# The last block of an expert layer moved into the head of the next block, with the layernorm and the turns done tile by tile

## The reference, cut to what matters

```python
# experts (end)
out = shared + acc @ Wup.T            # shared = (x2 @ sw1.T * sqrelu(x2 @ swg.T)) @ sw2.T
x = x + out
# linear attention (start)
h = _layernorm(x)                     # (x - mean) / sqrt(var + 1e-5), per token
qkv = silu(h @ qkv_w.T)               # 32 heads of 64, q, k, v
gate = sigmoid(h @ gate_w.T)
...
```

## Time and profile before

| | |
|---|---|
| median of 3 runs | 2136.52 us (2131.28 to 2137.3) |
| the profiled execution's own time | 2135.23 us |
| its span, first to last instruction | 2133.4 us |
| PE busy | 1935.3 us (91% of the span) |
| DVE busy | 1168.6 us (55%) |
| ACT busy | 635.2 us (30%) |
| POOL busy | 219.6 us (10%) |

### The profile page before, as it was taken

One profiled execution on the slowest core, in us unless ns is written; L12 is line 12 of the kernel. 1 busy time (PEld: TensorE's weight loads), 2 busy tenths in 40 slices (PEclk: granted clock), 3 DMA queues, 4 the chain that ended last, 5 costly groups with the idle time before them and its releaser, 6 DMA issues. The chain is left out here.

```text
span 2133.4 us, 24875 instructions
## 1 busy us (share of the span) xinstructions
PE 1935.3 (91%) x9621; PEld 1409.3 (66%) x9624; DVE 1168.6 (55%) x2069; ACT 635.2 (30%) x1013; POOL 219.6 (10%) x185
## 2 busy tenths in 40 slices
PE   7899795899997599979999999999899998899996
PEld 6677783444433458847886886877758744688885
DVE  5412737555543345547674684665643378656653
ACT  3311322444444055514340331322224221222110
POOL 0000001111201100000120120210200001112221
PEclk9999896899998599999999999999999999999998
DMA  5100402222210500014221313203202100110101
GB/s 198 40 1 0 158 11 67 67 68 58 64 37 1 158 0 1 1 36 140 77 79 66 114 54 116 97 20 117 80 31 70 60 20 22 58 37 25 39 1 40
DMA packets 67125, 124.12 MB, mean 58 GB/s; under 512 B 8512, under 2 KB 26944, under 8 KB 65472
## 3 DMA queue, kind: packets, MB, share of 16 engines
q1 hardware_dynamic: 67008, 122.53, 18.1%
HBM read 88.82 MB, written 14.68 MB: 49 GB/s over the span
## 5 line engine op out<-in xcount | busy, mean ns | idle before, releaser
L941 DVE TENSOR_REDUCE b_nm<-ps 128x1 f32<-128x1024 f32 x128 | 151.5, 1220 | 118.8 <-PE ps L862 118.8
L929 ACT ACTIVATE b_pr<-ps 128x512 f32<-128x512 f32 x256 | 132.3, 605 | 159.5 <-PE ps L880 159.5
L229 PE MATMUL ps<-d_x_high,d_w_high 128*128 128x512 f32 x384 | 154.8, 403 | 4.4 <-DVE d_w_low L1767 4.4
L230 PE MATMUL ps<-d_x_low,d_w_high 128*128 128x512 f32 x384 | 150.4, 392 | 0.0
L231 PE MATMUL ps<-d_x_high,d_w_low 128*128 128x512 f32 x384 | 150.3, 392 | 0.0
L892 PE MATMUL ps<-b_pr,b_VS 128*64 128x512 f32 x512 | 130.6, 634 | 0.0
L1544 PE MATMUL ps<-d_wo,d_ga 128*128 128x512 f32 x256 | 110.6, 593 | 1.5 <-DVE d_ga L1745 1.5
L880 PE MATMUL ps<-b_qS,b_kS 98*128 98x512 f32 x256 | 92.3, 442 | 20.1 <-DMA b_qS<-b_nm_parts 17.7
L862 PE MATMUL ps<-b_kS,b_qS 96*128 96x512 f32 x256 | 95.0, 461 | 15.6 <-DMA b_qS<-b_q_parts 10.1
L880 PEld LDWEIGHTS ps<-b_qS,b_kS 98*128 98x128 f32 x256 | 44.1, 192 | 90.7 <-issue 52.1
L1659 POOL TENSOR_TENSOR d_sqsum<-d_sqsum,d_sq 128x512 f32<-128x512 f32 x32 | 42.4, 1325 | 487.4 <-ACT d_sq L1604 487.2
(11 more groups left out here) (372 smaller groups left out, 4592.5 us busy)
## 6 DMA issues: line engine op xcount, KB each, us to landing
b_kS<-b_k_parts SPq DMA_DIRECT2D x96, 128.0 KB, 2.3
f_rows<-d_fw SPq DMA_DIRECT2D x24, 512.0 KB, 3.0
f_w<-f_rows SPq DMA_DIRECT2D x12, 1024.0 KB, 4.8
b_qS<-b_q_parts SPq DMA_DIRECT2D x96, 64.0 KB, 2.0
a_convT<-in_convT SPq DMA_DIRECT2D x4, 1024.0 KB, 12.8
b_ctxT<-in_ctxT SPq DMA_DIRECT2D x8, 512.0 KB, 5.1
d_w<-in_d_wq SPq DMA_DIRECT2D x16, 256.0 KB, 4.4
d_w<-in_d_wk SPq DMA_DIRECT2D x16, 256.0 KB, 4.3
```

What stands on the lines that cost most here:

```text
L229: nc.tensor.matmul(out, lhsT[0], rhs[0], start=start, stop=False)
L230: nc.tensor.matmul(out, lhsT[0], rhs[1], start=False, stop=False)
L929: nc.scalar.activation(pr[:, n % RING, :], c.ps[:, 4 + n % BANKS, :], ACT.Exp).then_inc(exp_done, 1)
L941: nc.vector.tensor_reduce(nm[:, g % 2, u:u + 1], c.ps[:, banks:banks + 2, :], AX.XY, ALU.max, negate=True).then_inc(job_read, 1)
```

## The change

Block 2 leaves `experts` and becomes the head of block 5. The blocks 3 and 4 vanish as blocks: their loads stand at the head of SP's list in block 5, and the layernorm is done by tile with `TileNorm`.

```diff
 experts():
-    a_turned, a_moved, out_done, added = (c.sem(f"c_{n}") for n in ("a_turned", "a_moved", "out_done", "added"))
-    with nc.Block() as block:
...
+    c.experts = acc, accF, sF, s2T, wupT
 linear_attention():
+    acc, accF, sF, s2T, wupT = c.experts
+    norm = TileNorm(c, "d_ln")
+    def x_bank(t):
+        return c.ps[:, 2 + t % 2, :].rearrange("p (k t) -> p k t", k=KD)
...
             sp.dma_start(nw[:], c.dram["d_nw"]).then_inc(in_c, 16)
-            pair_weights(sp, 0)
-            group_values(sp, 0)
-
-    norm_and_split(c, "d_ln", *x_parts)
-
-    with nc.Block() as block:
-        @block.sync
-        def _(sp):
             for p in range(PAIRS):
-                if p >= 1:
-                    pair_weights(sp, p)
+                pair_weights(sp, p)
...
                     if g == 0:
                         sp.dma_start(wo[:], tiled(c.dram["d_woT"])[:, 0:GP, :]).then_inc(in_o, 16)
+                        sp.wait_ge(out_done, TT)
+                        group_values(sp, 0)
...
         @block.tensor
+            def turn_x(t):
+                pe.wait_ge(norm.normed, t + 1)
+                if t >= 2:
+                    pe.wait_ge(x_low, t - 1)
+                for k in range(KD):
+                    last = nc.tensor.transpose(x_bank(t)[:, k, :], c.xn[:, t, k * P:(k + 1) * P], c.ident[:])
+                last.then_inc(x_turned, 1)
+            def experts_output(t):
...
             def project(j, i, n):
+                if j < 2:
+                    pe.wait_ge(x_low, 4 * (n + 1))
...
-            queries_keys(0, 0, 4)
+            for n in range(2):
+                for i in range(4):
+                    last = nc.tensor.transpose(c.ps[:, n, i * P:(i + 1) * P], acc[:, 4 * n + i, :], c.ident[:])
+                last.then_inc(acc_turned, 1)
+            for t in range(TT):
+                experts_output(t)
+                if t >= 2:
+                    turn_x(t - 2)
+            queries_keys(0, 0, 1)
+            turn_x(TT - 2)
+            turn_x(TT - 1)
+            queries_keys(0, 1, 4)
             gates(0)
             values(0)
         @block.scalar
+            for n in range(2):
+                act.wait_ge(acc_turned, n + 1)
+                nc.scalar.activation(accF[:, n * BANK:(n + 1) * BANK], c.ps[:, n, :], ACT.Copy).then_inc(acc_moved, 1)
             for i in range(3):
                 high_weights(0, i)
+            for t in range(TT):
+                act.wait_ge(x_turned, t + 1)
+                nc.scalar.activation(tile_of(x_parts[0], t), x_bank(t), ACT.Copy).then_inc(x_high, 1)
             high_values(0)
             pair(0)
         @block.gpsimd
+            for t in range(TT):
+                norm.root_pool(pool, t)
         @block.vector
             for i in range(3):
                 low_weights(0, i)
+            for t in range(TT):
+                dve.wait_ge(out_done, t + 1)
+                nc.vector.tensor_tensor(c.x[:, t, :], c.ps[:, 4 + t % 4, :], c.x[:, t, :], ALU.add).then_inc(added, 1)
+                dve.wait_ge(added, t + 1)
+                norm.measure_dve(dve, t)
+                if t >= 1:
+                    norm.scale_dve(dve, t - 1)
+                if t >= 3:
+                    low_x(t - 3)
+            norm.scale_dve(dve, TT - 1)
+            for t in range(TT - 3, TT):
+                low_x(t)
+            round_weights(2)
             low_values(0)
             for i in range(3):
                 low_weights(1, i)
-            round_weights(2 * UNITS_FIRST)
+            round_weights(2 * UNITS_FIRST - 2)
```

More of the change, by code:

```diff
@@ L1391, in group_values, with tile_of @@
         sp.dma_start(wv[:], tiled(c.dram["d_wvT"])[:, :, g * DM:(g + 1) * DM]).then_inc(in_v, 16)
+    acc, accF, sF, s2T, wupT = c.experts
+    acc_turned, acc_moved, out_done, added = (c.sem(f"c_{n}") for n in ("acc_turned", "acc_moved", "out_done", "added"))
+    x_turned, x_high, x_low = (c.sem(f"d_{n}") for n in ("x_turned", "x_high", "x_low"))
+    norm = TileNorm(c, "d_ln")
+    def tile_of(part, t):
+        return part[:, :, t * P:(t + 1) * P]
+    def x_bank(t):
+        return c.ps[:, 2 + t % 2, :].rearrange("p (k t) -> p k t", k=KD)
     with nc.Block() as block:
@@ L1451, in _ @@
         def _(pe):
+            def turn_x(t):
[6 more added lines that the diff above has]
+            def experts_output(t):
+                pe.wait_ge(acc_moved, 1 + t // 4)
+                if t >= 4:
+                    pe.wait_ge(added, t - 3)
+                for k in range(2):
+                    nc.tensor.matmul(c.ps[:, 4 + t % 4, :], sF[:, k, t * P:(t + 1) * P], s2T[:, k, :],
+                                     start=k == 0, stop=False)
+                nc.tensor.matmul(c.ps[:, 4 + t % 4, :], accF[:, t * P:(t + 1) * P], wupT[:], start=False,
+                                 stop=True).then_inc(out_done, 1)
             def project(j, i, n):
@@ L1772, in low_values, with low_x @@
                 nc.vector.tensor_tensor(wv_parts[1][:], wv[:], wv_parts[0][:].bitcast(F32), ALU.subtract).then_inc(wv_low, 1)
+            def low_x(t):
+                dve.wait_ge(x_high, t + 1)
+                nc.vector.tensor_tensor(tile_of(x_parts[1], t), x_bank(t), tile_of(x_parts[0], t).bitcast(F32),
+                                        ALU.subtract).then_inc(x_low, 1)
             for i in range(3):
                 low_weights(0, i)
+            for t in range(TT):
[11 more added lines that the diff above has]
+            round_weights(2)
             low_values(0)
```

## The result

| | before | after |
|---|---|---|
| median of the runs made side by side | 2133.9 us (4 runs, 2130.99 to 2137.3) | 2118.45 us (4 runs, 2117.53 to 2120.57) |
| ratio, with its 95% interval | | 0.9919 (0.9903 to 0.9936) |
| the profiled execution's own time, its span | 2135.23, 2133.4 us | 2120.57, 2118.7 us |
| PE busy | 1935.3 us | 1932.7 us |

The kernel is faster by 15.5 us between the medians; the forecast was a gain of 15.0 us, on the other median of before. The two profiled executions are 14.7 us apart in their spans.

What follows compares the result with a forecast made beforehand. PE was taken as the bound, with waits of 13.2 and 4.4 us before the projections. 14.2 us earlier at `values(0)` plus 0.8 gave 15.0 us: 2120.2 on the profiled execution, 2121.5 as median; range 2115 to 2129 us.

Steps and rivals of the forecast that it cites:

- Block end: At the merged block's start: SP and PE begin 0.9 us after DVE's last addition, costing 0.6 us.
- DVE's start: Before the first addition to x: pair 0's weights' loads and low parts delay it to 932.8 us, from near 929.
- PE's first wait: Before tile 0's turn, behind tile 2's output: PE waits 2.7 us for the scaling, in place of 13.2.
- The steady part: Interleaved outputs and turns: 3.0 us per output and turn, DVE wants 2.8, plus 0.5 us for close waits.
- The margin: Interleaved tiles: the needed scaling and low part come from DVE's round t-1, in time with 0.2 us to spare.
- The late load: Before projection 2: `d_wv` lands 6.4 us after issue, ACT's work behind it makes PE wait 1.6 us.
- The low part of `d_wv`: On DVE behind one 8.1 us unit of quantising: ends at 969.1 us, hidden with 4.9 us to spare before `values(0)`.
- Behind `values`: At DVE's first mask product: two quantising units remain instead of three, so PE's 0.8 us loss vanishes.
- given back later: Rival after `values(0)`: loads or quantising that don't move along lose 1 to 4 us of the gain; chance 0.05.
- low clock in a rival: Rival: PE's clock falls in the interleaved part; partly, 2 to 8 us, chance 0.08; for all of it, 2142.8 us, 0.05.
- the prediction's own sign: Wrong if the interleaved stretch's clock is below 1, outputs stand 4 us apart, or `values(0)` waits for `d_wv`'s low part.
- The account: Stretch up to `values(0)`: 25.0 us removed (waits, 1.7 low clock), 11.0 paid (barrier, late start, turns, waits, ACT).

Runs made afterwards that it cites:

- x_wv_late: The changed kernel with the value weights' load issued behind pair 1's five loads instead of ahead of them; 2125.78 us, ratio 0.9955 to the kernel before.
- x_low_late: The changed kernel with pair 0's weights' low parts moved from ahead of DVE's first addition to behind later tiles; run twice, 2112.04 and 2113.5 us.
- x_order: x_low_late with queries and keys of the first half projected before the second half, ACT and DVE work reordered to match; 2113.17 us, ratio 0.9900.
- x_merge: The changed kernel with blocks merged, but layernorm done for all eight tiles at once and turns behind all outputs; 2123.92 us, ratio 0.9952.
- x_turns_one: The changed kernel with turns one tile behind the outputs in place of two; 2151.15 us, ratio 1.0085 to the kernel before.

## Why the prediction was right, point by point

- **The gain.** 15.0 us forecast, 15.5 measured between medians. 2118.45 lies 3.1 us below the forecast, and 2.6 of that are the median of before, which came out at 2133.9 beside it in place of 2136.5. That it is so close is in part luck: the sum left out 1.7 us of low clock and put 1.3 too much on the late load, and the one pair of profiles gives 14.6 us at the stage's end.
- **Block end.** PE started 0.9 us after the last addition, as said.
- **DVE's start and PE's first wait.** From the loop's end to the first addition 8.6 us forecast, 8.9 and 9.9 measured; PE's wait 2.7 forecast, 2.8 and 3.8 measured (4.0 in x_wv_late, with the same code there). The mechanism held, and x_low_late, which takes it away, showed its worth: 5.0 us in the medians.
- **The steady part.** 3.0 us and 0.5 in all for small waits forecast, 3.1 us for each tile measured, at a clock of 1.00. The margin that the prediction read from the order of instructions was real: at a distance of two tiles nobody waits for long, at one tile everybody does.
- **The late load.** 1.6 us in front of projection 2 forecast, 0.3 measured (961.74 - 958.71 = 3.03, a projection is 2.73). The chain is right, as x_wv_late showed; the term was mis-sized, since `d_wv` landed in 5.3 us and I had taken the median of its other landings, 6.4.
- **The low part of `d_wv`.** Forecast to be hidden with 4.9 us to spare, measured 1.8 (ends at 970.9, `values(0)` at 972.71). DVE came to the unit of quantising 2.0 us later than said, and the unit took 10.2 us, not 8.1. The 8.1 was read where GpSimd was idle. In the changed kernel the unit's slow operations overlap GpSimd's product; so it is in x_low_late and x_order. No run moves the product alone, so that the cause is not shown. In x_order this low part is what PE waits for.
- **Behind `values`.** The 0.8 us vanished, and nothing was given back later.
- **The clock: the step that was wrong.** I summed the stretch at a clock of 1.00 and kept low clock in a rival: 2 to 8 us of it at a chance of 0.08. In the changed kernel's two profiles it cost 1.7 and 3.4 us. By the prediction's own sign (wrong if the clock in that stretch is below 1) this step failed, though the time came out. So the 1.7 us that I counted as removed with the slow projections was moved, to the output behind PE's first wait. In the stretch this stands as 50.7 us against 49.8 forecast: 1.7 for the clock, 0.3 for DVE's later start, 1.3 less for the late load, and 0.2 in small pieces. At the stage's end the first profile shows a gain of 14.6 us (652.2 - 637.6), the second one 11.7 (652.2 - 640.5). The medians give 15.5 with spells elsewhere mixed in: the second profile reached the end of the experts' loop 4.2 us before the first (917.8 against 922.0), in code that is the same. The evidence that I put against the rival was busy stretches with gaps below 1 us and one pause of 1.5 us; the pauses that the change leaves are 2.8 and 2.1 us, between those and the 4.4 of the earlier trace rows, and I decided for the nearer side without a row for it. Nor do show the clock behind the wait of 13.2 us, only within it; the window of the turns, below this list, does. The page that spoke for the rival, of the Trainium skill "TensorE: Matmul & The Clock Gate", section "A second HAM failure mode: psum-queue depth-cycling", ties the changes of the clock to short idle times between groups that rotate through the banks of PSUM. This trace neither bears it out nor refutes it: from 939.7 to 954 us, in four rounds through the banks, the clock is 1.00, but PE is busy for 14.21 of the 14.30 us there. The low spells stand behind longer waits.
- **The account.** 25.0 us removed, 11.0 paid came close as a sum, since the low clock put at nothing and the late load put too high nearly cancel. What it hid is that the tile-by-tile work, the larger part of the edit, was worth about a third of the gain or less as it was written (5.5 of 15.5 us in medians, 3.2 and 0.9 in the profiles: x_merge), since its cost stood in the same place: three low parts of weights ahead of DVE's first addition, and the first turn early in PE's list.

The turns of the kernel before, as a window (columns of the earlier trace rows):

```profile
960.00:965.70 5.70, 5.63 (x32) 5.39 (x32) 5.70 (x12) 3.73 (x7) 0.00 (x0) 0.65 0.00 0
```

What decides whether a spell of low clock follows a pause stays open. In the eleven profiles PE pauses thirteen times for 2.8 us or more in this stretch, and twelve of the pauses have low clock behind them (the exception is a pause of 3.06 us in x_turns_one, at 985.72, with a turn of 0.63 us behind it). A pause of 2.37 us in x_turns_one had one too. After the 2.1 us at the block's start it came in three of ten and stayed out in seven, after pauses of 1.5 to 1.8 us in two of nine. No experiment here sets a pause alone, so that this is a count and not a cause shown.

## What to carry to other kernels

When stages are merged and work is interleaved, look at what stands ahead of the first dependent instruction on the engine that feeds the others. Here three small operations, whose loads could only start at the merge, held back DVE's first addition and cost some 5 us, since PE's list wanted DVE's first result early; moved behind it, or with the turns moved behind all outputs, they cost no wait. A distance in a software pipeline is safe when the awaited instruction ends in an earlier round of the other engine: one tile less turned a gain of 0.8% into a loss of 0.85%. And price a longer wait of PE with the low clock behind it: here a wait of 2.8 us cost 4.5.

## What the runs showed of the hardware that I had not expected

- A spell of low clock cost the same wherever it stood in this stretch, 1.7 us when PE had work all through it; windows laid around such spells show a granted clock of 0.57 to 0.65, the level of 1.2 GHz with its edges. Its place changed from one execution of the same kernel to the next: at the block's start in one profile of x_low_late, nowhere in the other.
- PE's pause at this block's start is 2.1 us in all ten profiles of the merged form, 0.9 of it behind DVE's last addition; before it was 1.49.
- The same 1 MB load landed in 5.3 us with pair 1's loads behind it, and 7.7 us after issue with them ahead of it (x_wv_late).
- A pair of DVE's operations took 1.9 us beside a product of GpSimd and 0.8 us without one.
